# Writing out the loop over the head groups of a fused four-layer kernel's first attention

## The chip, the cores and the metric

The kernel runs on one core of a Trainium2 chip. The metric is the device time of one execution in microseconds, the median of several runs. Below, PE is the matrix engine TensorE (PEld its loading of weights), DVE is VectorE, ACT is ScalarE, POOL is GpSimd and SP is SyncE, which here only issues transfers.

## What is computed

The input is x, 4 sequences of 256 tokens with 512 features, all in float32. Six sublayers follow each other, each a normalisation and a residual addition around it:

```python
x = x + 0.5 * L0_ffn(layernorm(x))     # 512 -> 2 x 512, silu gate, -> 512
x = x + L0_attn(layernorm(x))          # the attention that the change touches
x = x + 0.5 * L0_ffn(layernorm(x))
x = x + 0.5 * L1_ffn(layernorm(x))     # low rank, 1376 wide
x = x + L1_attn(layernorm(x))
x = x + 0.5 * L1_ffn(layernorm(x))
```

The first attention is two attentions over the same queries, added:

```python
q = (x @ w_q)                          # 32 heads of 128
k, v = (x @ w_k), (x @ w_v)            # 8 heads of 128, each shared by 4 query heads
lq = x @ w_lq                          # 512 -> 128
lk, lv = (lq @ w_lk), (x @ w_lv)       # 32 heads of 128
q, k, lk = rope(q), rope(k), rope(lk)
out = causal_attn(q, k, v) @ w_o + causal_attn(q, lk, lv) @ w_lo
```

## The kernel before, in words

The program is written by hand, engine by engine: five functions, one for each engine and one for SP, run through the six sublayers, and the engines meet only at semaphores. Every wait has a number worked out in advance from the place in the work. The order in which each engine's instructions stand in the program is the order in which it runs them.

Weights come from memory in chunks of 128 x 512 floats (256 KB). SP loads each into one of four raw buffers (`Stream.load`, L245 to L250). ACT rounds a chunk to the format that PE multiplies (`split_hi`, L256), DVE takes the remainder (`split_lo`, L262; POOL does it in some places, L269), and a product is three matmuls on these parts (`product`, L357, used for all projections and scores). SP may load into a raw buffer again when the chunk before it there has been split, so the transfers are paced by DVE's semaphore w_split.

The first attention runs over 8 head groups (KVH = 8). A group has one key/value head, four query heads and 19 chunks of weights. Its work is cut into 16 steps, 4 batches times 4 heads. A step is a pipeline stage: it makes the scores of its own head, turns and weighs the probabilities of the head one step before, multiplies the result of the head two steps before by the output weights, and projects the query of the head two steps ahead. So a turn of the loop does not start at step 0. `a0_run` (L838 to L850) runs steps 0 and 1 of the first group, then a loop of KVH - 1 = 7 turns over steps 2 to 17, in which steps 16 and 17 are the next group's steps 0 and 1, and then steps 2 to 17 of the last group, written out. The loop is a loop of the hardware program (`eng.Fori`): the body stands in each engine's program once, a register counts the turns, and at the end of the body the engine jumps back six times. Numbers that depend on the group are computed from that register, among them the values that waits compare against (`inst`, `fill`, `rope` of class Step; `turn * self.n` of class Stream). In `Step` the flags first, second and last_group are only set where the group is a plain number; in the groups 0 to 6 from step 2 on they are false either way.

What each engine does in a step is in `a0_tensor_step`, `a0_scalar_step`, `a0_vector_step` and `a0_gpsimd_step`. The names that matter here:

- PE: the transposes of probabilities (L961, three per head and half), the weighted sums of values (L974, L976), products (L357). At steps with h == 0 (4, 8, 12, 16) it projects the values of a batch at the end of the step (`a0_values`, 48 matmuls in a row); at steps 2, 6, 10 and 14 it projects keys. Step 14 waits for the chunks C_K, C_Q and C_LK of the next group's weights (`WEIGHTS_FOR`, `weights`), the last of which is split late in step 13 (`SPLIT_LATE`).
- ACT: copies of transposed probabilities (L1086), exponentials (L1079), results (L1091), the rotation's swap and rounding (L1064, L1065, L1070).
- DVE: the rotation's products and sums (L1170, L1179), row minima (L1191, L1193), reciprocals (L1201), the remainder of the results (L1206), copies of the values (L1213), the additions to x (L1248) and the splits of weights (L262).
- POOL: L1278, L1286 (rotation), L1297, L1299 (normalisation).
- SP: within the loop it loads the 19 chunks of a turn, from an address computed from the turn's register; after it, the chunks of the second feed-forward.

The weights of the loop lie in memory in the order of their loading, so that the 19 chunks of turn g stand behind those of turn g - 1.

Of the kernel before, what the change touches and what calls it, by code (L numbers as in the profile page):

```python
# [35 lines left out]
HEADS0, KVH, HD = 32, 8, 128  # L36
GH = HEADS0 // KVH
G_CHUNKS = 19
# [9 lines left out]
BEFORE = TURN[OWN:]  # L48
# [30 lines left out]
W_A0 = W_LQ + 1  # L79
# [54 lines left out]
def program(nc, x_in, w_in, table_in, bias_in, rows_in, out):  # L134
    ctx = ExitStack()
    with ctx:
# [145 lines left out]
        st_loop = Stream(G_CHUNKS, KVH - 1)  # L282
# [557 lines left out]
        def a0_run(eng, step, other_half):  # L840


            step(Step(0, 0))
            other_half()
            step(Step(0, 1))
            with eng.Fori(0, KVH - 1) as g:
                for s in range(2, STEPS0 + 2):
                    step(Step(g, s))
            for s in range(2, STEPS0 + 2):
                step(Step(KVH - 1, s))  # L850
# [31 lines left out]
        def a0_tensor(pe):  # L882
            def turn_tiles(tiles):
                for t in tiles:
                    ln_turn(pe, 8 + t, t - 4, OUTB[t % 2], normed, 2)

            def other_half():
                turn_tiles((6, 7))
                pe.wait_ge(ln_done, 16)
                a0_latent(pe, 1)  # L890
                pe.wait_ge(a_lq_lo, 2)

            pe.wait_ge(f_mul, 2 * M0)
            st_a0.ready(pe, BEFORE.index(C_Q + 3))
            a0_keys(pe, Step(0, -2))
            pe.wait_ge(a_lq_lo, 1)
            a0_queries(pe, Step(0, -2))
            a0_queries(pe, Step(0, -1))
            turn_tiles((4, 5))
            a0_run(pe, lambda st: a0_tensor_step(pe, st), other_half)  # L900
# [134 lines left out]
        def a0_scalar(act):  # L1035
            def latent_hi(i):
                act.wait_ge(a_lq, i + 1)
                nc.scalar.copy(lqT[HI][:, i * CH:(i + 1) * CH], bank[LQB[i]][:, :]).then_inc(a_lq_hi, 1)

            def tiles_hi(tiles):  # L1040
                for t in tiles:
                    ln_hi_part(act, 8 + t, OUTB[t % 2], xn_tile(t))

            def other_half():
                tiles_hi((6, 7))
                latent_hi(1)

            latent_hi(0)
            a0_swap(act, Step(0, -2), "k")
            a0_swap(act, Step(0, -2), "q")  # L1050
            a0_rope_hi(act, Step(0, -2), "k")
            a0_rope_hi(act, Step(0, -2), "q")
            a0_swap(act, Step(0, -1), "q")
            a0_swap(act, Step(0, 0), "q")
            tiles_hi((4, 5))
            a0_run(act, lambda st: a0_scalar_step(act, st), other_half)
# [63 lines left out]
        def a0_vector(dve):  # L1120
# [37 lines left out]
            a0_cosine(dve, Step(0, -1), "q")  # L1158
            moments((6, 7))
            a0_run(dve, lambda st: a0_vector_step(dve, st), other_half)  # L1160
            dve.wait_ge(a_added, 1 + KVH * TILES)
            dve.sem_inc(x_written, 1)

        def a0_cosine(dve, st, what):
            n, s = st.rope(what)
            _, fs = st.fill(what)
            cols = st.columns(what)
            dve.wait_ge(a_swapped, n + 1)
            dve.wait_ge(a_rope_lo, n + 1)
            nc.vector.tensor_tensor(work[:, 2 + s, cols], bank[fs][:, cols],  # L1170
                                    table[:, T_COS + cols.start:T_COS + cols.stop],
                                    ALU.mult).then_inc(a_proj_free, 1)
# [9 lines left out]
        def a0_vector_step(dve, st):  # L1182
            before = st.near(-1)

            def minima(k):
                _, s = st.inst(k)
                if k == 0:
                    dve.wait_ge(a_scores, st.number() + 1)
                    dve.sem_inc(passed, 1)

                nc.vector.tensor_tensor_reduce(s0[:, s, 0:P], score_columns(k, 0), table[:, T_M0:T_M0 + P],  # L1191
                                               1.0, 3e38, ALU.add, ALU.min, neg_max[:, s, 0:1])
                nc.vector.tensor_tensor_reduce(s0[:, s, P:3 * P], score_columns(k, 1),  # L1193
                                               table[:, T_M0 + P:T_M0 + 3 * P],
                                               1.0, 3e38, ALU.add, ALU.min,
                                               neg_max[:, s, 1:2]).then_inc(a_min, 1)
# [636 lines left out]
        @block.sync  # L1833
        def _(sp):
            def flat(n):
                return w_in[n, :, :]

            xr = x_in.rearrange("(t p) d -> t p d", p=P)
            sp.dma_start(x[:, 0, :], xr[0]).then_inc(x_loaded[0], 16)
            sp.dma_start(table[:, 0:T_FIRST], table_in[:, 0:T_FIRST]).then_inc(table_loaded, 16)  # L1840
            sp.dma_start(biases[:, :], bias_in).then_inc(table_loaded, 16)
            for t in range(1, 4):
                sp.dma_start(x[:, t, :], xr[t]).then_inc(x_loaded[t], 16)
            for j in range(F0_CHUNKS):
                st_f0a.load(sp, j, flat(W_F0A + FIRST[j]))
                if j == 3:
                    for t in range(4, TILES):
                        sp.dma_start(x[:, t, :], xr[t]).then_inc(x_loaded[t], 16)
                    sp.dma_start(row[:, :], rows_in[0]).then_inc(row_loaded, 16)
            st_lq.load(sp, 0, flat(W_LQ))  # L1850
            rest = range(T_FIRST, T_ALL + 1, (T_ALL - T_FIRST) // 4)
            for j in range(len(BEFORE)):
                st_a0.load(sp, j, flat(W_A0 + j))
                if j in (2, 5, 8, 11):
                    at = slice(rest[j // 3], rest[j // 3 + 1])
                    sp.dma_start(table[:, at], table_in[:, at]).then_inc(table_rest, 16)
            with sp.Fori(0, KVH - 1) as g:
                for j in range(G_CHUNKS):
                    src = w_in[bass.ds(g * G_CHUNKS + (W_A0 + len(BEFORE) + j), 1), :, :]
                    st_loop.load(sp, j, src.rearrange("a p n -> (a p) n"), g)  # L1860
            for j in range(len(TAIL)):
                st_tail.load(sp, j, flat(W_F1 - len(TAIL) + j))
            sp.wait_ge(x_written, X1)
            sp.dma_start(row[:, :], rows_in[0]).then_inc(row_loaded, 16)
            for j in range(F1_CHUNKS):
                st_f1a.load(sp, j, flat(W_F1 + j))
            sp.wait_ge(x_written, X3)
            sp.dma_start(row[:, :], rows_in[1]).then_inc(row_loaded, 16)
            sp.dma_start(b_qk[:, :], rows_in[3:5].rearrange("a p n -> p a n")).then_inc(b_qk_loaded, 16)
            for j in range(A1_CHUNKS):  # L1870
                st_a1.load(sp, j, flat(W_A1 + j))
            sp.wait_ge(x_written, X4)
            sp.dma_start(row[:, :], rows_in[2]).then_inc(row_loaded, 16)
            sp.dma_start(b_val[:, :], rows_in[5]).then_inc(b_val_loaded, 16)
            for j in range(F1_CHUNKS):
                st_f1b.load(sp, j, flat(W_F1 + LAST[j]))
            sp.wait_ge(x_written, X5)
            sp.dma_start(row[:, :], rows_in[1]).then_inc(row_loaded, 16)
            outr = out.rearrange("(t p) d -> t p d", p=P)
            for t in range(TILES):  # L1880
                sp.wait_ge(x_written, ffn1b.added(t))
                sp.dma_start(outr[t], x[:, t, :]).then_inc(stored, 16)
            sp.wait_ge(stored, 16 * TILES)
# [114 lines left out]
```

## Time and profile before

| | us |
|---|---|
| median of 3 runs | 1891.56 (1889.14 to 1893.09) |
| the profiled execution, its time | 1892.9 |
| its span, first to last instruction | 1891.1 |
| mean granted clock of PE | 0.983 of full |
| PE busy | 1765.6 (93%) |
| DVE, ACT, POOL busy | 1124.1, 1086.6, 906.7 |
| transfers | 66.19 MB, mean 35 GB/s |

The profile records one execution. Its page gives busy times per engine, the span in 40 slices with the granted clock, the DMA queues, the chain of waits that ended last and the costliest groups of instructions. Register, branch, semaphore and DMA-issuing instructions are not counted as busy. "issue" is time in which an engine waited for nothing that the profile shows. The trace behind the page can be cut: windows (busy time of each engine in a stretch), waits (who waited for whom), the timeline of single instructions, and the DMA queues. Program code reaches the engines through two DMA queues named instruction, q8 and q14. In this execution the loop of the first attention begins before 162 us and the last group ends near 1400 us.

### The profile page before, as it was taken

Reading aid. Unit: us, or ns where it says so; the run is one execution under the profiler, and the core shown is the slowest. Engines: PE = TensorE matmul, PEld = TensorE weight load, DVE = VectorE, ACT = ScalarE, POOL = GpSimd, SP = SyncE. Lnnn points to the kernel's source line nnn. Section 1 sums busy time; section 2 is a strip of 40 time slices with the busy share of each in tenths; the row PEclk is TensorE's granted clock in tenths of the full one; section 3 lists DMA queues with packets and bytes.
Section 4 is the critical chain, followed back from the end, with each engine's and each line's share of the span. In section 5 each row is a group of like instructions: output and inputs, shape, how many; then the busy total and the mean of one; then the engine's idle time right before and its main releaser. Section 6 shows DMA issues by size and latency. Waiting matters only on the chain.

```text
span 1891.1 us, 34627 instructions
## 1 busy us (share of the span) xinstructions
PE 1765.6 (93%) x11076; PEld 1530.7 (81%) x11076; DVE 1124.1 (59%) x3334; ACT 1086.6 (57%) x3071; POOL 906.7 (48%) x1153
## 2 busy tenths in 40 slices
PE   7979999999999999999999999999989788898788
PEld 5769988988998898898899989899968566666566
DVE  5655565556546546545655654664566767677656
ACT  3336565566547556556655655664642445777854
POOL 4445544555545455444555445454423326668720
PEclk9989999999999999999999999999989998999999
DMA  3300021012002101101200110110011200000001
GB/s 124 111 23 18 7 64 39 1 36 68 7 18 59 33 1 57 53 1 35 62 13 18 57 36 1 46 62 1 29 56 28 90 31 20 2 1 24 18 7 45
DMA packets 35462, 66.19 MB, mean 35 GB/s; under 512 B 4032, under 2 KB 4672, under 8 KB 35264
## 3 DMA queue, kind: packets, MB, share of 16 engines
q1 hardware_dynamic: 35264, 63.73, 11.0%
q8 instruction: 102, 1.67, 0.4%
q14 instruction: 96, 0.79, 0.1%
HBM read 61.62 MB, written 2.10 MB: 34 GB/s over the span
## 4 chain that ended last, share of the span: by engine, by line
PE 69%; DVE 9%; issue 8%; ACT 8%; POOL 5%; DMA 0%; DVEq 0%; SPq 0%; ACTq 0%; POOLq 0%
PE bank L357 54%; PE bank L974 5%; PE bank L961 4%; PE bank L976 3%; ACT s L1079 2%; POOL s L1795 1%; PE bank L1510 1%; PE bank L1481 1%; PE bank L1497 1%; DVE h L676 1%; POOL WF L269 1%; ACT s L1566 1%; ACT W L256 1%; POOL W L269 1%; POOL rstd L322 1%
## 5 line engine op out<-in xcount | busy, mean ns | idle before, releaser
L357 PE MATMUL bank<-W,oT 128*128 128x512 f32 x1632 | 433.2, 402 | 1.0 <-DVE oT L1747 1.0
L1286 POOL TENSOR_TENSOR qk<-work,qk 128x512 fp32r<-128x512 f32 (+1 forms) x160 | 191.5, 1197 | 469.0 <-ACT qk L1070 469.0
L357 PEld LDWEIGHTS bank<-W,oT 128*128 128x128 f32 x1632 | 290.3, 190 | 49.3 <-issue 1.3
L1086 ACT COPY pt<-bank 128x384 f32<-128x384 f32 x256 | 122.0, 477 | 338.8 <-PE bank L961 338.5
L1278 POOL TENSOR_TENSOR work<-work,table 128x512 f32<-128x512 f32 (+1 forms) x160 | 192.1, 1201 | 139.2 <-ACT work L1065 139.2
L1079 ACT ACTIVATE s<-s,neg_max 128x128 f32<-128x128 f32 (+1 forms) x512 | 227.7, 446 | 49.5 <-DVE neg_max L1193 48.7
L357 PE MATMUL bank<-W,xnA 128*128 128x320 f32 (+1 forms) x1056 | 186.5, 333 | 3.1 <-DVE xnA L342 2.8
L357 PEld LDWEIGHTS bank<-W,xnA 128*128 128x128 f32 x1056 | 166.9, 188 | 16.6 <-DVE xnA L342 4.0
L1170 DVE TENSOR_TENSOR work<-bank,table 128x512 f32<-128x512 f32 (+1 forms) x160 | 101.9, 637 | 128.7 <-ACT work L1065 128.7
L357 PE MATMUL bank<-xnA,W 128*128 128x256 f32 (+1 forms) x1080 | 162.7, 301 | 8.0 <-DVE W L262 6.6
L357 PE MATMUL bank<-xnB,W 128*128 128x256 f32 (+1 forms) x1080 | 165.9, 304 | 3.3 <-DVE xnB L342 3.3
L974 PE MATMUL bank<-pt,lvv 128*128 128x256 f32 x512 | 154.0, 382 | 14.9 <-DVE oT L1206 14.2
L357 PE MATMUL bank<-qk 128*128 128x256 f32 (+1 forms) x768 | 166.0, 351 | 0.0
L1213 DVE COPY lvv<-bank 128x320 f32<-128x320 f32 x128 | 62.9, 491 | 168.5 <-PE bank L357 168.5
L1299 POOL TENSOR_TENSOR s<-s,inv_sum 128x256 f32<-128x256 f32 x256 | 157.8, 616 | 0.0
L357 PEld LDWEIGHTS bank<-xnA,W 128*128 128x128 f32 x1080 | 143.3, 191 | 17.3 <-DVE W L262 9.6
L357 PEld LDWEIGHTS bank<-xnB,W 128*128 128x128 f32 x1080 | 146.0, 193 | 10.7 <-DVE xnB L342 4.0
L1795 POOL TENSOR_TENSOR s<-s,b_inv_sum 128x384 f32<-128x384 f32 x128 | 113.5, 907 | 61.7 <-DVE b_inv_sum L1714 61.5
L1179 DVE TENSOR_TENSOR work<-work 128x512 f32<-128x512 f32 (+1 forms) x160 | 116.0, 725 | 43.0 <-POOL work L1278 28.7
L1070 ACT CAST qk<-work 128x512 fp32r<-128x512 f32 (+1 forms) x160 | 92.3, 577 | 85.4 <-DVE work L1179 84.8
L961 PE MATMUL bank<-table,s 128*128 128x128 f32 x768 | 125.9, 273 | 10.4 <-issue 9.0
L1297 POOL TENSOR_TENSOR s<-s,inv_sum 128x128 f32<-128x128 f32 x256 | 108.0, 422 | 46.0 <-DVE inv_sum L1201 46.0
(106 smaller groups left out, 3516.7 us busy)
## 6 DMA issues: line engine op xcount, KB each, us to landing
raw<-in_weights SPq DMA_DIRECT2D x215, 256.0 KB, 2.8
x<-in_x SPq DMA_DIRECT2D x8, 256.0 KB, 5.9
out<-x SPq DMA_DIRECT2D x8, 256.0 KB, 2.1
row<-in_bias_rows SPq DMA_DIRECT2D x5, 256.0 KB, 2.7
table<-in_constants SPq DMA_DIRECT2D x4, 240.0 KB, 3.6
b_qk<-in_bias_rows SPq DMA_DIRECT2D x1, 512.0 KB, 3.8
b_val<-in_bias_rows SPq DMA_DIRECT2D x1, 256.0 KB, 3.0
table<-in_constants SPq DMA_DIRECT2D x1, 66.0 KB, 2.3
```

What stands on the lines that cost most here:

```text
L357: last = nc.tensor.matmul(out_ap, lhs(i), rhs(j), start=start and k == 0, stop=stop and k == 2)
L961: last = nc.tensor.transpose(bank[PT][:, blk * P:(blk + 1) * P], s0[:, s, blk * P:(blk + 1) * P], ident)
L974: nc.tensor.matmul(bank[OB][:, 0:SEQ], lvv[:, 0, col:col + P], pt0[:, k, 0:2 * P], start=True, stop=False)
L1079: last = nc.scalar.activation(s0[:, s, cols], s0[:, s, cols], ACT.Exp, bias=neg_max[:, s, qt:qt + 1], scale=-1.0, accum_out=row_sum[:, s, ...
L1086: nc.scalar.copy(pt0[:, k, :], bank[PT][:, 0:3 * P]).then_inc(a_pt, 1)
L1170: nc.vector.tensor_tensor(work[:, 2 + s, cols], bank[fs][:, cols], table[:, T_COS + cols.start:T_COS + cols.stop], ALU.mult).then_inc(a_pr ...
L1179: nc.vector.tensor_tensor(work[:, 2 + s, cols], work[:, 2 + s, cols], work[:, s, cols], ALU.add).then_inc(a_rope, 1)
L1278: nc.gpsimd.tensor_tensor(work[:, s, cols], work[:, s, cols], table[:, T_SIN + cols.start:T_SIN + cols.stop], ALU.mult).then_inc(a_sin, 1)
L1286: nc.gpsimd.tensor_tensor(lo, work[:, 2 + s, st.columns(what)], hi.bitcast(F32), ALU.subtract).then_inc(a_rope_lo, 1)
L1297: nc.gpsimd.tensor_tensor(s0[:, s, 0:P], s0[:, s, 0:P], inv_sum[:, s, 0:1].to_broadcast([P, P]), ALU.mult)
L1299: nc.gpsimd.tensor_tensor(s0[:, s, P:3 * P], s0[:, s, P:3 * P], inv_sum[:, s, 1:2].to_broadcast([P, 2 * P]), ALU.mult).then_inc(a_norm, 1)
L1795: nc.gpsimd.tensor_tensor(blocks, blocks, b_inv_sum[:, at, 1:4].unsqueeze(2).to_broadcast([P, 3, P]), ALU.mult).then_inc(b_norm, 1)
```

## The change

Both `Fori` loops become Python loops: the body of 16 steps stands seven times in the program of each of the four compute engines, with the group as a plain number, and SP's 19 loads stand seven times with plain addresses. The order on each engine, the semaphores and the values that are waited for stay as they were. No register is computed, and no engine jumps back between the groups.

```diff
@@ -843,7 +843,7 @@
             step(Step(0, 0))
             other_half()
             step(Step(0, 1))
-            with eng.Fori(0, KVH - 1) as g:
+            for g in range(KVH - 1):
                 for s in range(2, STEPS0 + 2):
                     step(Step(g, s))
             for s in range(2, STEPS0 + 2):
@@ -1854,10 +1854,9 @@
                 if j in (2, 5, 8, 11):
                     at = slice(rest[j // 3], rest[j // 3 + 1])
                     sp.dma_start(table[:, at], table_in[:, at]).then_inc(table_rest, 16)
-            with sp.Fori(0, KVH - 1) as g:
+            for g in range(KVH - 1):
                 for j in range(G_CHUNKS):
-                    src = w_in[bass.ds(g * G_CHUNKS + (W_A0 + len(BEFORE) + j), 1), :, :]
-                    st_loop.load(sp, j, src.rearrange("a p n -> (a p) n"), g)
+                    st_loop.load(sp, j, flat(W_A0 + len(BEFORE) + g * G_CHUNKS + j), g)
             for j in range(len(TAIL)):
                 st_tail.load(sp, j, flat(W_F1 - len(TAIL) + j))
             sp.wait_ge(x_written, X1)
```

## Rows read from the trace of the kernel before

**Rows 1.** The page: span, busy time, granted clock in 40 slices, chain by engine.
```profile
span 1891.1 us, 34627 instructions
PE 1765.6 (93%) x11076; PEld 1530.7 (81%) x11076; DVE 1124.1 (59%) x3334; ACT 1086.6 (57%) x3071; POOL 906.7 (48%) x1153
...
PEclk9989999999999999999999999999989998999999
...
PE 69%; DVE 9%; issue 8%; ACT 8%; POOL 5%; DMA 0%; DVEq 0%; SPq 0%; ACTq 0%; POOLq 0%
```

**Rows 2.** Windows: length, busy us (count) of PE, PEld, DVE, ACT, POOL, clock, DMA share, GB/s.
```profile
162.04:321.70 159.66, 155.92 (x994) 142.32 (x993) 89.10 (x276) 96.33 (x271) 78.73 (x105) 1.00 0.11 33
958.67:1117.63 158.96, 155.93 (x994) 142.33 (x993) 89.10 (x276) 96.32 (x271) 78.73 (x105) 1.00 0.10 33
162.04:1117.63 955.59, 935.58 (x5954) 853.91 (x5953) 534.59 (x1651) 577.95 (x1626) 472.57 (x625) 1.00 0.11 33
1117.63:1274.21 156.58, 155.64 (x993) 142.40 (x993) 88.19 (x276) 96.32 (x271) 79.36 (x105) 1.00 0.11 33
```

**Rows 3.** Windows, the same columns: boundary quarters of turns 1, 6, 7, then the last group.
```profile
279.68:321.70 42.02, 39.22 (x250) 35.49 (x249) 24.87 (x74) 26.06 (x72) 20.03 (x27) 1.00 0.20 58
1076.32:1117.63 41.31, 39.21 (x250) 35.49 (x249) 24.83 (x73) 26.03 (x72) 20.02 (x27) 1.00 0.18 59
1235.28:1274.21 38.93, 38.93 (x249) 35.56 (x249) 23.98 (x74) 26.05 (x72) 20.62 (x27) 1.00 0.21 62
1274.21:1313.02 38.81, 38.81 (x249) 35.60 (x249) 18.95 (x65) 21.61 (x63) 19.52 (x27) 1.00 0.00 1
1313.02:1351.84 38.82, 38.82 (x250) 35.64 (x249) 20.30 (x67) 22.51 (x65) 19.36 (x26) 1.00 0.02 8
```

**Rows 4.** Windows of two other quarters of the loop; a wait of step 14.
```profile
239.67:279.68 40.01, 39.07 (x249) 35.55 (x249) 25.02 (x74) 26.06 (x73) 19.84 (x26) 1.00 0.21 61
321.70:360.51 38.81, 38.81 (x249) 35.63 (x249) 18.95 (x65) 21.67 (x63) 19.55 (x27) 1.00 0.00 1
...
PE bank L357 <- DVE W L262: 4.7, 5, 0.9
```

**Rows 5.** Waits of PE over 280 to 1120 us: total us, times, longest.
```profile
PE bank L961 <- issue: 9.0, 6, 1.7
PE bank L974 <- DVE oT L1206: 5.4, 6, 1.2
```

**Rows 6.** Timeline around the first edge: start us, us, engine, line, then idle time before.
```profile
297.27 0.52 PE L961 MATMUL bank<-table,s 128*128 128x128 f32 x3 [1.58 <-issue]
...
305.65 0.67 PE L974 MATMUL bank<-pt,lvv 128*128 128x256 f32 x2 [1.21 <-DVE oT L1206]
...
300.10 0.69 DVE L1179 TENSOR_TENSOR work<-work 128x512 f32<-128x512 f32 x1 [2.76 <-issue]
...
298.11 0.48 ACT L1086 COPY pt<-bank 128x384 f32<-128x384 f32 x1 [2.62 <-PE bank L961]
```

**Rows 7.** Timeline of DVE at the seventh boundary.
```profile
1252.85 0.69 DVE L1179 TENSOR_TENSOR work<-work 128x512 f32<-128x512 f32 x1
```

**Rows 8.** DMA queues (packets, MB) in 290:301, 1246:1257 and 321.70:480.72.
```profile
q8 instruction: 2, 0.03, 1.4%
q14 instruction: 4, 0.03, 0.9%
...
q8 instruction: 1, 0.02, 0.7%
...
q8 instruction: 10, 0.16, 0.4%
q14 instruction: 10, 0.08, 0.2%
```

**Rows 9.** Timeline of DVE: the late split of step 13, in the loop and written out.
```profile
257.24 0.69 DVE L262 TENSOR_TENSOR W<-raw,W 128x512 fp32r<-128x512 f32 x1
...
1369.41 0.69 DVE L262 TENSOR_TENSOR W<-raw,W 128x512 fp32r<-128x512 f32 x1
```

## The prediction, made before the changed kernel was run

> **What bounds the kernel now.** I read the page first [rows 1]. TensorE (PE) is busy for 93% of the span and the chain that ended last lies on it for 69%. That makes it the engine to follow, but an average over stages does not say what the loop costs. So I cut the span at one mark that comes once per batch in the first attention, the start of a block of value projections, which shows as the widest piece of the chain of waits. From the mark of step 4 of one head group to that of the next is one turn of the loop, edge included. The windows view [rows 2] has 159.66 us for the first turn, 158.96 for the sixth, 955.59 for the first six together (the four between lie between these two), and 156.58 us for the seventh, with the same instruction counts (PE x993 or x994, DVE x276, ACT x271, POOL x105), the same DMA rate (33 GB/s) and the clock granted in full (1.00). The seventh turn ends where the loop ends: behind its step 17 comes step 2 of the last group, which is written out already, so no engine jumps back.
>
> Cutting finer [rows 3], the whole difference sits in the quarter that holds steps 17 and 2: 42.02 us in turn one, 41.31 in turn six, 38.93 in the seventh. The quarter behind it takes 38.81 us, in the written-out last group (and the next one there 38.82) [rows 3] as in the loop [rows 4]; the quarter that ends a turn before the edge takes 40.01 us in the loop [rows 4], and PE waits in it once, for a split of weights on DVE, which I come back to.
>
> The waits of PE over six turns name what it is at the edge [rows 5]: before the first transposes of step 2 (L961) it idles 9.0 us in six, "issue", which is idle time that no semaphore explains; then, before the weighted sum of values (L974), 5.4 us in six for the result parts of VectorE (L1206). The timeline around the first edge shows how these hang together [rows 6]. PE's transposes of step 2 begin at 297.27 after 1.58 us in which it did nothing. VectorE (DVE) stands for 2.76 us until 300.10, "issue" again; ScalarE's (ACT) first copy of the step is at 298.11 after 2.62 us idle. The exponentials and the copy of the second transposes (L1086) run late because of that, and PE, which was first held by its own edge, is held once more at 305.65 for 1.21 us. At the seventh boundary PE is busy for all of the 38.93 us [rows 3], and DVE starts the same rotation at 1252.85 with no idle time before it [rows 7].
>
> What stops the engines can be read from the instruction queues [rows 8]: in 11 us around the first edge they bring six pieces of program (two of 16 KB on q8, four of 8 KB on q14), around the seventh boundary, same length and same place in the step, one. I read it so: at each edge the engines wait for code that has to be fetched anew. The Trainium skill says the same ("Runtime: NRT & Kernel Launch", Instruction fetch mechanics: a taken branch whose target is not in the small window of code held forces a DMA fetch before the engine goes on); by that rule, the trace agrees.
>
> **The change, part by part.**
>
> *The six backward jumps go.* Six turns take 955.59 us [rows 2]. Without the edge each should take what the seventh takes: 6 x 156.58 = 939.48. The term is **-16.1 us**. A cross-check from the quarters [rows 3]: 42.02 - 38.93 = 3.09 us at the first edge, 41.31 - 38.93 = 2.38 at the sixth, which is what those turns as wholes are over the seventh (3.08 and 2.38). A second one from the waits: 9.0 + 5.4 us idle on PE, and the quarters with an edge hold some 39.2 us of PE busy time against 38.93 [rows 3], 6 x 0.3 = 1.7 more, since the pipeline runs dry and fills again; together 16.1. All of it is on the path, because PE is never idle in the quarters of the seventh boundary: what PE loses at an edge is not caught up.
>
> *The loop's register work goes.* In the loop every wait with the group number needs its value computed and compared from a register; those instructions are not counted as busy. Bound: the quarter in the loop that has no edge takes 38.81 us [rows 4], the same quarter written out 38.81 [rows 3]. So 0 on the path; PE, which is always busy there, hides it. The other end is a gain where PE does wait: step 14 waits for DVE's split of the latent weights (L262), 40.01 - 39.07 = 0.94 us idle and 40.01 - 38.81 = 1.2 us in the length of the quarter [rows 4], once in each of seven turns. That split starts at 257.24 in the loop, 17.57 us behind the mark of its quarter at 239.67; in the written-out last group the split at this place starts at 1369.41, 17.57 us behind the mark at 1351.84 [rows 9]. The written-out code is not earlier, so I take 0; the far end, 7 x 1.2 = 8.4 us gained, stays a rival.
>
> *Longer straight code.* Each of six more copies is fetched by the instruction queues. A turn brings ten 16 KB pieces and ten 8 KB pieces [rows 8], so most of the loop body is already fetched anew every turn and the traffic hardly changes. That straight code costs nothing is shown by the seventh boundary and the quarter behind it, which lie in the written-out group: 38.93 and 38.81 us, PE busy for all of both [rows 3]. Where POOL and SP do hold their short loops now, which no row decides, they would have to fetch more; POOL is busy for 79 of a turn's 159 us and the transfers that SP issues take 0.11 of the DMA engines [rows 2], and this slack hides it. If the cover were gone, a fetch would cost what it costs PE and DVE at the first edge, 1.58 to 2.76 us [rows 6].
>
> *Order, waits and transfers* are as they were. The weight chunks are paced by DVE's splits through four raw buffers (the wait in Stream.load), not by SP's loop. What was late at the edge because of the edge (L974) goes with it. What is late next is the step-14 wait, which stays with its 0.94 us in all seven turns.
>
> *Behind the attention* everything starts 16.1 us earlier and otherwise unchanged. The row of the granted clock has slices at 0.8 there, while it is full all through the loop [rows 1, 2]; those are mixtures of 2.4 and 1.2 GHz, and where a drop falls against the work may shift. Bound: the runs of before differ by 3.95 us (1889.14 to 1893.09), so I allow 2 us either way.
>
> **Sum.** The profiled execution took 1892.9 us (span 1891.1 and 1.8 around it): 1892.9 - 16.1 = 1876.8. It lies 1.3 us above the median, 1891.56; from the median, which is what is to be compared, 1891.56 - 16.1 = **1875.5 us** (0.9% less).
>
> **The rivals.**
> 1. *Only PE's own edge counts.* The idle 9.0 us goes, but the late DVE and ACT stay, for instance since their first instructions of step 2 wait for other work: 1891.6 - 9.0 - 1.7 = about 1881. For it: the second wait [rows 5] bears another engine's name. Against: at the seventh boundary ACT and DVE are on time. 4%.
> 2. *The edge is cheap and the idle time is not its own.* Something in the boundary from step 17 to 2 would hold PE anyway, such as the additions to x on DVE and the weight transfers that fall there: 1891.6, no change. Against: the seventh boundary has the same instructions and transfers (58 against 62 GB/s [rows 3]) and no stall. 2%. The Trainium skill ("Advanced Engine Details and Errata", Control Flow Timing) has a compare-and-branch at about 108 ns; six of them would be 0.65 us and the time 1890.9. The trace shows more: DVE alone stands 2.76 us at the first edge.
> 3. *More than the edges:* without register work DVE's split at step 14 comes early enough and that wait closes as well: 1875.5 - 8.4 = 1867. Against: the equal 17.57 us. 3%.
> 4. *Slower: straight code falls behind the weight loads.* PE's code arrives in pieces of 16 KB, about every 16 us, on DMA engines that carry 256 KB weight chunks in bursts in steps 12 to 17 and 2 to 3. If each copy now meets one or two pieces late, at the 1.58 us of PE's idle time and the 1.21 of the wait behind it [rows 6], that is 2.8 us each, where an edge cost 2.7. To lose what is won takes 16.1 / 2.8 = six late pieces in seven copies; at ten the kernel is at 1891.6 + 28 - 16.1 = 1903.5, and from eight on it is measurably slower. Against: the seventh boundary ran straight through such a burst at 62 GB/s in 38.93 us. 2%.
> 5. The change does what it says, with an unknown smaller than the edges: the forecast itself, 89%.
>
> **How the numbers follow.** The likeliest case gives 1875.5. Its own spread is that of medians of three (about 1.5 us either way), of the clock behind the attention (2 us) and of 0.3 us per turn by which the seven could differ (2 us): 1871.5 to 1879.5. Rivals 1 to 4 hold 11% and lie outside; the range may leave out 20%, so it needs no stretching to them: 1871.0 to 1880.0. A measurement of this kernel can tell about 0.2% (3.8 us) from no change. Faster by more: the forecast, rivals 1 and 3, 0.96. Within it: rival 2, 0.02. Slower: rival 4, 0.02.
>
> **What the profile after would show.** Right: the seven turns all 156.6 us long between the same marks; the quarters of the boundary 38.9 each; no "issue" before L961 in the attention and none before DVE's L1179; PE waiting for DVE's L1206 there not at all; the 0.94 us before L357 of step 14 unchanged, seven times; instruction queues with about as much as before. Rival 1: boundary quarters of some 39.9 us with the wait at L974. Rival 2: the same 41.3 to 42.0. Rival 3: the quarter before at 38.8. Rival 4: "issue" on PE at places that move from copy to copy. A boundary quarter above 39.5 us, or a stage behind the attention that is over 3 us off, would prove me wrong.

## The result and the profile after

| | before | after |
|---|---|---|
| median, us (6 runs each) | 1892.16 (1888.97 to 1895.40) | 1878.62 (1872.54 to 1881.21) |
| ratio to before, 95% interval | | 0.9923 (0.9902 to 0.9944) |
| profiled execution, us | 1892.9 | 1872.54 |
| its span, us | 1891.1 | 1870.7 |

The kernel became 0.8% faster, 13.5 us by the medians, and 1878.62 lies within the range forecast (1871 to 1880, 1875.5 named). The profiled execution of after is its fastest, so the 20.4 us between the two spans say too much. How much of them belongs to the loop is read between the same marks as before. The first fence is the windows view of the changed kernel, with the columns of [rows 2] and [rows 3]: turn one, turns one to six together, turn seven; then the boundary quarters of turns one, two and seven.

```profile
157.52:314.54 157.02, 155.75 (x994) 142.17 (x993) 88.84 (x276) 96.36 (x271) 78.90 (x105) 1.00 0.11 33
157.52:1098.51 940.99, 934.33 (x5954) 853.78 (x5953) 528.43 (x1651) 578.17 (x1626) 476.59 (x625) 1.00 0.11 33
1098.51:1255.31 156.80, 155.72 (x993) 142.31 (x993) 88.10 (x276) 96.45 (x271) 79.53 (x105) 1.00 0.11 33
275.36:314.54 39.18, 39.09 (x250) 35.47 (x249) 24.53 (x73) 25.97 (x72) 20.07 (x27) 1.00 0.21 61
432.18:471.33 39.15, 39.01 (x250) 35.52 (x249) 24.54 (x73) 25.96 (x72) 20.08 (x27) 1.00 0.21 62
1216.15:1255.31 39.16, 39.02 (x249) 35.52 (x249) 24.54 (x73) 25.98 (x72) 20.08 (x27) 1.00 0.20 61
```

The stretch from the first of these marks to the last took 955.59 + 156.58 = 1112.17 us before and takes 940.99 + 156.80 = 1097.79 us now: **14.4 us less**, about what the measured ratio gives (0.77% of 1892.16 is 14.6 us). Six turns gave back 14.6, not the 16.1 of the forecast, and the seventh, which had no edge before either, became 0.22 us longer. The rest of the difference lies ahead of the first mark and behind the last, in code that did not change. The next fence has these two stretches before, then after, and then those of a variant of the same code there (ACT's loop alone, below); the column behind POOL is the granted clock as a share of full.

```profile
0.00:162.04 162.04, 134.90 (x670) 112.25 (x671) 96.67 (x195) 69.20 (x150) 78.05 (x86) 0.96 0.26 80
1274.21:1891.10 616.89, 539.46 (x3463) 422.18 (x3462) 404.62 (x1215) 343.13 (x1024) 276.74 (x340) 0.96 0.09 27
```

```profile
0.00:157.52 157.52, 132.02 (x670) 110.12 (x671) 94.90 (x195) 69.38 (x150) 78.68 (x86) 0.97 0.26 82
1255.31:1870.70 615.39, 537.92 (x3463) 420.82 (x3462) 403.93 (x1215) 343.38 (x1024) 277.33 (x340) 0.96 0.08 27
```

```profile
0.00:160.22 160.22, 134.76 (x670) 112.30 (x671) 95.69 (x195) 69.51 (x150) 78.58 (x86) 0.96 0.26 81
1259.34:1881.30 621.96, 546.40 (x3464) 429.24 (x3462) 404.43 (x1215) 343.96 (x1024) 276.76 (x340) 0.94 0.09 27
```

Over the executions of this study the beginning took 157.5 to 162.4 us and the end 612.4 to 622.3; the same instructions met a mean granted clock of 0.97 in the shortest end and of 0.94 in the longest. Turns in which no engine with a long body stops at an edge took 156.5 to 157.2 us in all of them, where the work at steps 2 and 14 was left as it is. So the experiments below are read from the **stretch** between the marks, not from whole times; each stretch comes from a single execution, and a difference of less than 1 us between two is not taken for a cost.

The waits of PE over 275 to 1120 us, the stretch that answers to [rows 5], hold one line, and it is the wait of step 14 that was to stay:

```profile
PE bank L357 <- DVE W L262: 4.7, 5, 0.9
```

Nothing is left of "issue" before L961, and of the wait for L1206 only 0.14 us a turn, too short for this view (the timeline below has it). The page's section on the DMA queues shows less program, not about as much: q8 carried 102 packets (1.67 MB) before, q14 96 (0.79 MB).

```profile
q8 instruction: 90, 1.47, 0.3%
q14 instruction: 70, 0.57, 0.1%
```

### The profile page after: what moved, and what is told of

It is laid out like the page before. It is cut to its first block, busy times and chain, and to the rows that moved or that the text cites. A ratio compares the mean times of both kernels' runs of the same rounds, so it can differ in the third digit from the quotient of the medians.

```text
span 1870.7 us, 32100 instructions
## 1 busy us (share of the span) xinstructions
PE 1760.0 (94%) x11076; PEld 1527.0 (82%) x11076; DVE 1115.4 (60%) x3334; ACT 1087.4 (58%) x3071; POOL 912.1 (49%) x1153
## 4 chain that ended last, share of the span: by engine, by line
PE 71%; DVE 9%; ACT 8%; issue 7%; POOL 5%; DMA 0%; SPq 0%; POOLq 0%; DVEq 0%; ACTq 0%
PE bank L357 55%; PE bank L974 5%; PE bank L961 4%; PE bank L976 3%; ACT s L1079 2%; POOL s L1795 2%; PE bank L1510 1%; PE bank L1481 1%; PE bank L1497 1%; DVE h L676 1%; ACT s L1566 1%; ACT W L256 1%; POOL WF L269 1%; POOL W L269 1%; POOL rstd L322 1%
## 5 line engine op out<-in xcount | busy, mean ns | idle before, releaser
L1299 POOL TENSOR_TENSOR s<-s,inv_sum 128x256 f32<-128x256 f32 x256 | 163.7, 640 | 0.0
L974 PE MATMUL bank<-pt,lvv 128*128 128x256 f32 x512 | 154.1, 382 | 10.3 <-DVE oT L1206 8.5
L961 PE MATMUL bank<-table,s 128*128 128x128 f32 x768 | 125.6, 273 | 1.4 <-DVE lqT L1128 1.4
L1179 DVE TENSOR_TENSOR work<-work 128x512 f32<-128x512 f32 (+1 forms) x160 | 111.2, 695 | 24.2 <-POOL work L1278 23.8
```

The lines of the kernel that those rows point to most:

```text
L961: last = nc.tensor.transpose(bank[PT][:, blk * P:(blk + 1) * P], s0[:, s, blk * P:(blk + 1) * P], ident)
L974: nc.tensor.matmul(bank[OB][:, 0:SEQ], lvv[:, 0, col:col + P], pt0[:, k, 0:2 * P], start=True, stop=False)
L1179: nc.vector.tensor_tensor(work[:, 2 + s, cols], work[:, 2 + s, cols], work[:, s, cols], ALU.add).then_inc(a_rope, 1)
L1299: nc.gpsimd.tensor_tensor(s0[:, s, P:3 * P], s0[:, s, P:3 * P], inv_sum[:, s, 1:2].to_broadcast([P, 2 * P]), ALU.mult).then_inc(a_norm, 1)
```

## The experiments

All stretches in one table, each from one profiled execution. A written-out engine has seven copies of the body, a looping one the hardware loop of before. The added lines of code shift the line numbers: in the kernels with one or two looping engines L961, L974, L976 and L1206 of before are L966, L979, L981 and L1211, and in the kernel with two jumps L961 is L964.

| kernel | stretch, us | over "after" | boundary quarters of turns 1 to 6, us |
|---|---|---|---|
| before (all five loop) | 1112.17 | 14.4 | 41.31 to 42.02 |
| after (none) | 1097.79 | 0 | 39.15 to 39.18 |
| only PE loops | 1105.29 | 7.5 | 40.20 to 40.72 |
| only DVE loops | 1118.03 | 20.2 | 41.47 to 43.32 |
| only ACT loops | 1099.12 | 1.3 | 39.07 to 39.70 |
| only POOL and SP loop | 1097.29 | -0.5 | 38.91 to 39.16 |
| PE and DVE loop | 1113.45 | 15.7 | 41.59 to 42.00 |
| none, but with registers | 1097.72 | -0.1 | 39.15 to 39.18 |
| turns 5 to 7 loop | 1103.82 | 6.0 | 39.15 to 39.17 in four, 41.77, 42.46 |
| all loop, jump hinted | 1098.04 | 0.3 | 39.15 to 39.20 |

**Which engine's jump costs.** The kernels of this part give `a0_run` a switch, and the engines named take the loop while the others are written out:

```diff
+            if looped:
+                with eng.Fori(0, KVH - 1) as g:
+                    for s in range(2, STEPS0 + 2):
+                        step(Step(g, s))
+            else:
                 for g in range(KVH - 1):
                     for s in range(2, STEPS0 + 2):
                         step(Step(g, s))
```

PE alone:

> Only PE keeps the hardware loop; ACT, DVE, POOL and SP are written out. Read from the first values mark of the loop to the mark of the last group's step 4 (1112.17 us before, 1097.79 after). Theory (each edge stops its own engine for a fetch, and PE's own stop is on the path): PE idles 1.2 to 1.8 us before L961 at six edges and not before L974, boundary quarters 40.4 to 41.0 us, stretch some 1107. Rival A (the edges of DVE and ACT cost what is lost, PE's idle time only runs beside them): the same idle time but nearly nothing lost, stretch under 1100. Rival B (an edge stops all engines together or costs the same whoever makes it): 1112.

Measured: 1105.29 us, with quarters of 40.20 to 40.72, two of them under the range; PE idles before the first transposes (L961, here L966) as before and nowhere else for a loop's sake. The waits of PE over 160 to 1266 us:

```profile
PE bank L966 <- issue: 8.6, 6, 1.7
PE bank L357 <- DVE W L262: 6.8, 7, 1.2
```

8.6 us of idle time and 7.5 lost: PE's own stop is on the path nearly whole. Rivals A and B fall.

DVE alone:

> Only DVE keeps the hardware loop. Theory: DVE stands 2.1 to 2.8 us before L1179 as it did; everything behind it on the chain to L974 of step 3 is late by that, and PE, which is no longer held by an edge of its own, waits there in one piece for what it used to wait in two: boundary quarters 41.2 to 42.0 us, stretch 1111 to 1114, nearly all of the loss though only one of five loops is left. Rival (the losses of the engines add up, 1.6 for PE and 1.1 for the others): quarters of 40.0 to 40.3, stretch 1104.

Measured: 1118.03 us, *more than with all five loops*. The theory had the direction and the place, but not the size. First the waits of PE over 162 to 1281 us, then one boundary quarter (turn 2) and the 3.5 us in it behind the stop:

```profile
PE bank L979 <- DVE oT L1211: 15.3, 6, 2.7
```

```profile
464.50:468.00 3.50, 3.13 (x9) 2.64 (x10) 3.33 (x5) 2.40 (x6) 2.99 (x4) 0.60 0.27 76
439.21:482.53 43.32, 40.62 (x250) 36.65 (x249) 24.77 (x73) 25.96 (x72) 19.97 (x27) 0.96 0.20 56
```

and how PE's timeline reads there:

```profile
464.87 0.86 PE L979 MATMUL bank<-pt,lvv 128*128 128x256 f32 x2 [2.70 <-DVE oT L1211]
465.52 0.63 PE L981 MATMUL bank<-pt,lvv 128*128 128x128 f32 x2
465.81 2.91 PE L357 MATMUL bank<-W,oT 128*128 128x512 f32 x6
468.51 0.55 PE L966 MATMUL bank<-table,s 128*128 128x128 f32 x3
```

Six matmuls that take 1.63 us elsewhere take 2.91 here. After 2.70 us in which PE did nothing, the granted clock stands at 0.60 of full over these 3.5 us, a mixture of 1.2 and 2.4 GHz; from 468.4 to 472.0 it is 0.97. It happened in four of six turns, with quarters of 43.0 to 43.3 us, behind stops of 2.51 to 2.70 us; the other two, with stops of 2.44 and 2.50 us and the clock full, took 41.47 and 41.50, as the theory had it. What decides between 2.50 and 2.51 us no run here shows. 15.3 us of idle time and four drops of some 1.6 us, less the 0.22 us per boundary that the written-out kernel loses at the same wait (below), are 15.3 + 6.4 - 1.3 = 20.4, about the 20.2 measured.

If that is right, PE's own loop must help. This was run with both:

> PE and DVE keep their loops, ACT, POOL and SP are written out. With DVE's loop alone the stretch was 1118.0 us, longer than with all five loops (1112.2): PE stopped once per edge for 2.5 to 2.7 us in one piece before L974 of step 3, and behind four of the six stops its granted clock was at 1.2 GHz for 3.4 us. Theory: PE's own edge cuts that stop into two, of 1.2 to 1.7 and 0.5 to 1.2 us, between which it works, and the clock stays full; so adding a loop makes the kernel faster: no slice of the loop below full clock, boundary quarters 41.3 to 42.0, stretch 1111 to 1113. Rival (the losses of PE and DVE add up): over 1118. Rival (the drops come from something else in the written-out ACT, POOL or SP): the clock drops here too.

Measured: 1113.45 us (0.45 above the range), no slice below full clock, quarters of 41.59 to 42.00. The windows and waits of the whole stretch:

```profile
157.81:1271.26 1113.45, 1091.26 (x6946) 996.31 (x6945) 623.44 (x1926) 674.30 (x1897) 551.43 (x729) 1.00 0.11 33
```

```profile
PE bank L966 <- issue: 8.6, 6, 1.6
PE bank L979 <- DVE oT L1211: 6.8, 6, 1.6
```

The idle time is about that of DVE's loop alone (15.4 us against 15.3), in twelve pieces instead of six: a loop added, 4.6 us won. That the cutting in two is what keeps the clock full is a reading; it rests on 12 edges with two pieces (six here, six in before) without a drop, against six in one piece, four of them with one. The kernel before is this case (9.0 + 5.4 us in [rows 5]), so DVE's jump sets its loss, 2.5 us a turn, and PE's stop lies inside that time. The two costs do not add.

ACT alone, and POOL with SP:

> Only ACT keeps the hardware loop. In the kernel before, ACT's first copy of step 2 (L1086) came 18.4 us behind the mark of the boundary quarter, without an edge 16.4; PE asks for it at about 18.6. Theory: ACT stands 2 us longer, most of it in time in which it would wait anyway, and PE loses what is left: boundary quarters 39.3 to 39.8 us, stretch 1098.5 to 1102. Rival (losses per edge are alike on the long bodies): as with DVE's loop, 41.5 us and more.

> Only POOL and SP keep their loops, whose bodies are short. Theory (a jump costs when its target must be fetched, and is cheap for a short body; both have slack): no idle time called issue on PE or DVE at the boundaries, quarters 38.9 to 39.2, stretch 1096.2 to 1098. Rival (a jump costs 2 to 4 us on any engine): POOL's first operation of the step, L1286, late by as much, and a loss of 1 to 2 us per edge, stretch 1104 to 1110.

Measured: 1099.12 us for ACT (quarters 39.07 to 39.70, the lowest a little under the range), and 1097.29 for POOL and SP, whose jumps cost nothing that can be seen. ACT stood for 2.3 to 2.7 us at its six edges; most of that passes before PE asks for what ACT makes, and some 0.2 us per edge reach PE.

**Registers without jumps.**

```diff
-            for g in range(KVH - 1):
+            regs = nc.alloc_registers(f"turn_{eng.engine}", engines=[eng.engine])
+            for turn in range(KVH - 1):
+                nc.regs_mov(regs, turn)
+                g = nc.snap(regs, min_val=0, max_val=KVH - 2)
```

> Everything written out, but on PE, ACT, DVE and POOL the group number is put into a register at the head of each of the seven copies, so all waits are computed from it as in the loop: the register work without any jump (SP is written out with plain numbers). Theory: register work costs nothing on the path, quarters without a boundary 38.81, stretch 1096 to 1098. The 0.22 us per turn by which the written-out kernel missed the seventh turn of before are put down to a race at step 2: POOL's L1299 and DVE's L1179 start within 10 ns of each other (POOL 8 ns later in the seventh turn of before, at the same time after), and whoever is second takes 0.3 to 0.5 us longer. With the registers back, POOL comes second again, DVE's L1179 takes 0.42 and the boundary quarter 38.93: stretch 1096.2. Rival (the 0.22 us come from longer code or its fetches, not from this race): quarters stay 39.15. Rival (register work was part of the gain): quarters over 39.2.

Measured: 1097.72 us. The register work costs nothing, as forecast. But the boundary quarters of the six copies that compute from registers stayed at 39.15 to 39.18, so my account of what decides the race was wrong; the seventh, which runs into the group without registers, took 38.92. More on it under the swapped order.

**Two jumps instead of six.**

```diff
-            for g in range(KVH - 1):
+            for g in range(4):
+                for s in range(2, STEPS0 + 2):
+                    step(Step(g, s))
+            with eng.Fori(4, KVH - 1) as g:
```

> Turns 1 to 4 written out on the four compute engines, turns 5 to 7 a loop (SP written out throughout): two backward jumps on each instead of six. Theory (the cost belongs to the jumps): boundary quarters of turns 5 and 6 take 41.3 to 42.0 us, the other five 38.9 to 39.2; stretch 1097.8 + 2 x 2.5 = 1102.8 (1101.5 to 1103.5). Rival (it belongs to being in a loop at all, registers included): turn 7 is longer as well.

Measured: 1103.82 us, 0.3 above the range; turn 7 is as short as the others (156.79), so the cost belongs to the jumps. The later quarter, 42.46 us, is above its range too. At both jumps PE's timeline shows something new, a second stop in the middle of a product; at the first jump:

```profile
920.49 0.52 PE L964 MATMUL bank<-table,s 128*128 128x128 f32 x3 [1.17 <-issue]
920.77 1.29 PE L357 MATMUL bank<-qk 128*128 128x256 f32 x6
921.89 0.76 PE L357 MATMUL bank<-xnA,W 128*128 128x256 f32 x5
924.08 0.99 PE L357 MATMUL bank<-xnA,W 128*128 128x256 f32 x7 [1.43 <-issue]
```

No wait stands between the fifth and the sixth matmul of those twelve. The body is the same as before but stands elsewhere in the program, and PE runs out of code a second time 3.6 us after the first. A piece of 16 KB on q8 lands at 918.71 and another at 922.72, before PE goes on at 920.49 and at 924.08. DVE's stops, 2.42 and 3.18 us, are here in part longer than in before (2.06 to 2.76). That the place of the loop's head among the fetched pieces decides it was not tried by itself.

**The same loops with the jump announced.** The kernel before, all loops in place, with one instruction at the head of the body that names the backward jump:

```diff
-            with eng.Fori(0, KVH - 1) as g:
+            with nc.Fori(0, KVH - 1, engines=[eng.engine], hint_back_edge=True) as g:
```

> The kernel before with all loops, and at the head of the body of PE, ACT, DVE and POOL one instruction that names the backward jump in advance, so that its target can be fetched before it is taken. Theory (the edge costs because the code of the target is fetched late): nearly all of the loss goes though all loops stay: no issue wait over 0.5 us on PE or DVE at the boundaries, boundary quarters 38.9 to 39.8 us, stretch 1096 to 1102. Rival (it costs whatever is held, by the jump itself or by the emptied instruction queue): quarters 41.3 to 42.0 and 1112 as before. Rival (the held target takes the room of the code that comes next): issue waits elsewhere in the body.

Measured: a stretch of 1098.04 us, and 1875.87 us for its one execution, beside 1896.83 for the kernel before on that chip (of these 21 us only 14.1 are in the stretch). The jumps are all still taken, and the stops are gone. What is left is the wait of step 14 and one gap of 0.42 us, in the last turn, where the announced jump is not taken. The window of the stretch, the wait and the gap:

```profile
159.92:1257.96 1098.04, 1090.17 (x6945) 996.79 (x6945) 622.02 (x1926) 675.22 (x1897) 552.30 (x729) 1.00 0.11 33
PE bank L357 <- DVE W L262: 6.6, 7, 0.9
...
1236.55 1.34 PE L357 MATMUL bank<-xnA,W 128*128 128x256 f32 x9 [0.42 <-issue]
```

This is the run that settles the mechanism: the edge costs because its target's code arrives late, not through the jump, the registers or the loop. It also reaches the gain of the change with one added instruction per engine instead of six more copies.

The transfers of program say the same. Which queue serves whom follows from the pages: q8 carries 102 pieces in each of the three kernels in which PE loops over all seven turns, and 90 where PE is written out with plain numbers (after, and DVE, ACT, or POOL and SP looping), so it is PE's, and a jump of PE costs two pieces more; DVE's loop adds 15 pieces on q14 to the 70 of after, ACT's adds 17, and that of POOL and SP takes 6 away. At each of PE's six stops in before, a piece on q8 had landed 1.6 to 2.0 us before PE went on, and with ACT's loop alone a piece on q14 1.3 to 1.5 us before ACT did. The next fence has the queues over the seven turns, first before, then with the jump announced:

```profile
q8 instruction: 69, 1.13, 0.4%
q14 instruction: 68, 0.56, 0.2%
```

```profile
q8 instruction: 64, 1.05, 0.4%
q14 instruction: 6, 0.05, 0.0%
```

PE's code is still fetched in every turn, but in time. On q14 nothing comes between 240 and 1247 us: with the jump announced, DVE, ACT and POOL run turns two to six without any transfer of program. So for these three the code does not come in time, it need not come at all.

**The race at step 2, and the wait of step 14.** The seventh turn grew by 0.22 us though it had no edge before either. Two timelines show where: those of DVE and POOL in the seventh boundary before, then those of DVE, POOL and PE in the second boundary after.

```profile
1257.01 0.42 DVE L1179 TENSOR_TENSOR work<-work 128x256 f32<-128x256 f32 x1
...
1257.02 0.89 POOL L1299 TENSOR_TENSOR s<-s,inv_sum 128x256 f32<-128x256 f32 x1
```

```profile
453.90 0.90 DVE L1179 TENSOR_TENSOR work<-work 128x256 f32<-128x256 f32 x1
454.73 0.41 DVE L1206 TENSOR_TENSOR oT<-bank,oT 128x256 fp32r<-128x256 f32 x1
...
453.91 0.61 POOL L1299 TENSOR_TENSOR s<-s,inv_sum 128x256 f32<-128x256 f32 x1
...
455.29 0.67 PE L974 MATMUL bank<-pt,lvv 128*128 128x256 f32 x2
```

Both engines begin within 10 ns of each other; the one that loses takes 0.3 to 0.5 us longer. Where DVE loses, L1206 behind it is late and PE starts L974 0.14 us after its matmuls before (which end at 455.15). The Trainium skill ("SBUF — State Buffer", Who interferes with whom) says that a DVE instruction with two SBUF inputs and a GpSimd instruction that reads SBUF contend for an exclusively held pair of ports, and that the second waits until the first is done. The trace agrees that one of the two is held up, but not with the length: by the rule the loser would take 0.42 + 0.61 = 1.03 us in all (an estimate), and it takes 0.89 or 0.90.

Who wins is not the registers' doing. With POOL and SP looping, DVE won in turns 1 and 3 and lost in the others; with registers it lost in all six, and with the announced loops, registers and all, too (quarters of 39.15 to 39.20). What decides it stays open. The swapped order takes the race off PE's path:

```diff
+            swapped = st.key and st.s == 2
-            if st.key:
+            if st.key and not swapped:
                 a0_rotate(dve, st, "k")
             if lagging(st):
                 result_lo(0)
+            if swapped:
+                a0_rotate(dve, st, "k")
```

> The written-out kernel with one change of order on DVE: at step 2 (and nowhere else) the remainder of the result (L1206), for which PE waits, comes ahead of the rotation's sum for the keys (L1179). In the runs so far the boundary quarter is 38.91 to 38.93 us where that L1179 took 0.42 us and 39.14 to 39.18 where it took 0.88 to 0.90, the latter when POOL's L1299 had started within 10 ns of it or before it. Theory: the length of L1179 reaches PE only through L1206 behind it; with the order swapped the quarters are 38.8 to 39.0 in all seven turns whatever L1179 takes, stretch 1095.5 to 1096.8. Rival (the rotation is as urgent: its later end makes PE wait elsewhere): 39.1 or more.

Measured: 1095.92 us, all seven quarters 38.86 to 38.89, with PE busy throughout. The theory holds. The second boundary quarter:

```profile
433.70:472.58 38.88, 38.88 (x250) 35.54 (x249) 23.76 (x73) 25.96 (x72) 20.58 (x27) 1.00 0.20 62
```

The wait of step 14 [rows 4], divided:

```diff
             if st.s in WEIGHTS_FOR:
-                weights(pe, st, WEIGHTS_FOR[st.s])
+                weights(pe, st, [C_K] if st.s == 14 else WEIGHTS_FOR[st.s])
...
+            if st.s == 14:
+                weights(pe, st, WEIGHTS_FOR[st.s])
             if st.queries and not st.first:
                 a0_queries(pe, st)
```

> The written-out kernel with one wait of PE divided: at step 14 the key projection waits for the split of the key chunk alone, and the wait for the latent chunk, split last on DVE, stands ahead of the query projection, some 3 us later in PE's order. Theory: the 0.9 to 1.2 us of idle time before the keys' products go, the quarter ahead of each boundary falls from 40.02 to 38.8 to 38.95 us, stretch 1097.8 - 7 x 1.2 = 1089.4 (1089 to 1091). Rival (DVE, ACT or POOL is late at step 14 by as much anyway, and PE waits for them a few operations on): the wait reappears before L974 or at the transposes of step 15, and the quarter stays above 39.5.

Measured: 1094.38 us, 3.4 us less instead of the 8.4 expected, with quarters ahead of the boundary of 39.49 to 39.78 instead of 40.02. The idle time before the keys' products is gone, but more than half of the gain is lost again a few operations later, as the rival had it:

```profile
261.90 0.67 PE L974 MATMUL bank<-pt,lvv 128*128 128x256 f32 x2 [0.51 <-DVE oT L1208]
```

DVE is behind at step 14 with all its work, not only with the split; with PE no longer held for the split, the remainder of the result (L1206, here L1208) is late next. The swapped order was only applied to step 2; step 14 was not tried with it.

**Both edits**, written out and in the loops with the hint, five executions each:

> The written-out kernel with both edits, the swapped order on DVE at step 2 and the divided wait on PE at step 14. They touch different steps, so they add: stretch 1086.8 to 1089, time about 1877.2 - 8.4 - 1.5 = 1867 us, 1863 to 1871, a ratio to the kernel before of 0.987. Rival (one edit takes the slack of the other): stretch over 1091.

> The kernel with its loops and the advance naming of the backward jump, and both edits. With the hint alone the stretch was 1098.0 us, the same as written out (1097.8). Theory: the same as the written-out kernel with both edits to within 1 us: stretch 1087 to 1090, time 1863 to 1871. Rival (the loop needs slack that the two idle times gave it): above 1872.

| | median, us | ratio to before | stretch, us |
|---|---|---|---|
| both, written out | 1871.94 (1869.21 to 1876.34) | 0.9896 (0.9877 to 0.9916) | 1092.87 |
| both, loops with hint | 1872.07 (1869.03 to 1880.13) | 0.9894 (0.9876 to 0.9913) | 1094.49 |

The kernel before took 1892.91 beside these. Both medians are below the changed kernel's 1878.62, which was measured at another time; the intervals of the ratios overlap with its 0.9902 to 0.9944, but the stretches, 4.9 and 3.3 us shorter, do not depend on that. The forecast of 1867 was too low by what the divided wait did not bring. Both stretches miss their ranges and the written-out one is over the rival's 1091, but not by the rival's cause: alone, the two edits bring 1.9 and 3.4 us, together 4.9. The kernels were to agree within 1 us and differ by 1.6, of which about 1.0 lies in the quarters ahead of the boundary (39.76 in all seven with the hint, 39.51 or 39.52 in four of seven written out); why is not known.

## Why the prediction was right, and where it was off

- *The bound and the cut* held. PE is the engine to follow in the loop, and the quarters without a boundary or a step 14 kept their 38.81 us.
- *The six jumps*: forecast -16.1 us, measured -14.4 over the stretch. The mechanism is shown by the hinted kernel. The step that was mis-sized is "without the edge each should take what the seventh takes". The seventh's 156.58 us was the lucky side of the race between DVE and POOL; the usual written-out turn takes 156.80. Seven times 0.22 us is 1.5 of the 1.7 us missing, and turn one, 0.22 longer than the others (its quarter ahead of the boundary took 40.22), is the rest. Turn one is taken up behind this list.
- *The cross-check came out at 16.1 by a term that was too large.* It counted 0.28 us per edge of extra PE busy time, against the seventh quarter's 38.93. The written-out quarters hold 39.01 us of busy time and 0.14 us idle at L974, so of 39.21 or so only 0.20 goes, and the 0.14 stays. That it agreed with the other sum was no second proof, since both took the seventh boundary as the rule.
- *One seventh turn was one sample.* Its edge-free quarter could not show that a second length existed. I had allowed 0.3 us per turn for it, which is what it needed.
- *How PE's two waits hang together* was told the wrong way round in part. The prediction has PE "first held by its own edge", then "once more". In truth DVE's stop alone costs as much as both (quarters of 41.5 where the clock stays full), and PE's stop lies inside it.
- *Register work at nothing*: right, on the path (1097.72 against 1097.79).
- *Straight code at nothing*: right in time but for the 0.12 us stop of DVE in turn one. That the traffic hardly changes was wrong: it fell by 0.42 MB of 2.46. The kernel with registers but no jumps carries 2.19 MB, so 0.27 of it went with the jumps and 0.15 with the register instructions. POOL's and SP's short loops cost nothing either way.
- *The step-14 wait stays*: right, seven times, 6.8 us in total.
- *Behind the attention*: 2 us either way was too little for a single execution. The end varied by 9.9 us over the kernels of this study, which share that code. With medians of six the total still came within 3.1 us of the forecast: 1.7 are the loop's, 0.6 the higher median of before, and about 0.8 lie in the code that did not change. That it fell inside the range was close: the range ends at 1880, and the interval of the ratio, on 1892.16, reaches from 1873.6 to 1881.6.
- *Rival 1* (1881) did not occur, since the change takes out DVE's jump too; had that stayed, nothing would have been gained, where the rival has 10.7 us: the kernel with DVE's loop alone shows it. *Rivals 2, 3 and 4* did not occur. The kernel with two jumps shows that a second late piece of code can cost 1.4 us, the thing rival 4 was built on; it was seen behind jumps alone.

In turn one of the changed kernel DVE's late split starts 17.84 us behind the mark at 235.14; in turn two it starts 17.57 us behind the one at 392.16:

```profile
252.98 0.68 DVE L262 TENSOR_TENSOR W<-raw,W 128x512 fp32r<-128x512 f32 x1
...
409.73 0.68 DVE L262 TENSOR_TENSOR W<-raw,W 128x512 fp32r<-128x512 f32 x1
```

Ahead of it DVE stands for 0.12 us at 245.54, for nothing that the trace shows, and PE's wait at step 14 grows from 0.94 to 1.18 us. Every kernel in which turn one of DVE is written out in plain numbers has this stop; those with a loop or registers on DVE do not. So straight code was not quite free. What the stop is stays open.

## What to carry to other kernels

An edge of a hardware loop with a long body costs the wait for the first instructions of the body, 1.2 to 3.2 us here on each engine that must fetch. The path loses only what the slowest chain through these engines loses, not the sum. Look first whether the loop can announce its jump: that brought the same as writing out all its turns. When one boundary in the trace lacks the cost, it is the best estimate there is of the rest, but it is a sample of one: look whether something beside it, such as two engines starting together, could as well have come out the other way.

## What was unexpected of the hardware

- Taking a loop away made the kernel slower. Against all five loops (1112.17 us), DVE's loop alone took 1118.03, with PE's idle time in one piece of 2.4 to 2.7 us and the granted clock at 1.2 GHz for part of the next 3.5 us in four of six cases; cut in two by PE's own stop, about the same idle time left the clock full in six of six.
- Two instructions that start within 10 ns decide over 0.25 us a turn by who comes first. The recorded starts do not tell who won: with DVE at 1257.01 and POOL at 1257.02 it was DVE, with 453.90 and 453.91 it was POOL.
- A turn entered by a jump can run out of code twice, 3.6 us apart, for 1.17 and 1.43 us.
- An announced jump did more than bring its target early: the transfers of program for DVE, ACT and POOL fell from 68 pieces over the seven turns to 6, fewer than the 40 of the written-out code.
